# GpSimd's block inversion one slot later, and N made by VectorE in four operations from the exponential

## What is computed

```python
def step(S, inp):
    qt, kt, vt, gt, bt = inp
    S = S * jnp.exp(gt)[:, None, None]
    kv = jnp.einsum('hk,hkv->hv', kt, S)
    delta = (vt - kv) * bt[:, None]
    S = S + kt[:, :, None] * delta[:, None, :]
    o = jnp.einsum('hk,hkv->hv', qt, S)
    return (S, o)
```

## Time and profile before

| | |
|---|---|
| median of 3 runs | 3036.22 us (3026.62 to 3046.79) |
| the profiled execution | 3028.94 us, span 3027.2 us |
| PE busy | 2794.9 us, 92% |
| VectorE busy | 2181.0 us, 72% |
| ScalarE busy | 1812.3 us, 60% |
| GpSimd busy | 1565.5 us, 52% |
| mean granted TensorE clock | 0.971 of full speed |

### The profile page before, as it was taken

One profiled execution on the slowest core, in us unless ns is written; L12 is line 12 of the kernel. 1 busy time (PEld: TensorE's weight loads), 2 busy tenths in 40 slices (PEclk: granted clock), 3 DMA queues, 4 the chain that ended last, 5 costly groups with the idle time before them and its releaser, 6 DMA issues. The chain is left out here.

```text
span 3027.2 us, 75586 instructions
## 1 busy us (share of the span) xinstructions
PE 2794.9 (92%) x24303; PEld 1909.6 (63%) x24303; DVE 2181.0 (72%) x4677; ACT 1812.3 (60%) x6310; POOL 1565.5 (52%) x3737
## 2 busy tenths in 40 slices
PE   5999489999999999999999999999999999869998
PEld 4556256666666666666666666666666666655555
DVE  3443468878877887877778778877788788547676
ACT  3321557777766776777677667766677677332332
POOL 1000456667666666666667666766666666410000
PEclk9999789999999999999999999999999999979999
DMA  3000132212222222212122212122222222110000
GB/s 88 1 1 0 28 59 40 45 38 45 42 48 43 49 43 44 49 35 49 35 49 42 54 37 51 39 46 38 45 40 52 42 49 42 24 42 1 8 7 15
DMA packets 485567, 113.74 MB, mean 38 GB/s; under 512 B 423296, under 2 KB 484336, under 8 KB 485168
## 3 DMA queue, kind: packets, MB, share of 16 engines
q1 hardware_dynamic: 485168, 108.76, 18.0%
HBM read 80.63 MB, written 28.06 MB: 36 GB/s over the span
## 5 line engine op out<-in xcount | busy, mean ns | idle before, releaser
L1216 DVE SCALAR_TENSOR_TENSOR S<-S,gs,bank 128x128 f32<-128x128 f32 x1024 | 287.3, 343 | 232.3 <-PE bank L776 228.0
L1247 DVE SCALAR_TENSOR_TENSOR conv<-raw,ckq,conv 128x512 f32<-128x512 f32 x384 | 302.2, 799 | 110.4 <-ACT conv L1001 104.1
L539 POOL TENSOR_TENSOR btmp<-Bk,Tb 64x14 f32<-64x14 f32 (+6 forms) x896 | 339.7, 379 | 66.1 <-POOL Tb L543 0.9
L543 POOL TENSOR_TENSOR Tb<-Tb,btmp 64x14 f32<-64x14 f32 (+6 forms) x896 | 315.2, 352 | 70.9 <-POOL btmp L539 1.3
L986 ACT ACTIVATE sq_gat<-gat 128x128 bf16<-128x128 f32 x512 | 151.8, 297 | 279.2 <-DVE gat L1232 279.2
L1247 DVE SCALAR_TENSOR_TENSOR conv<-raw,cv,conv 128x512 f32<-128x512 f32 x384 | 291.6, 772 | 12.2 <-ACT conv L1001 7.3
L528 POOL TENSOR_TENSOR Tb<-Bk,lower 64x256 f32<-64x256 f32 x64 | 56.0, 875 | 434.8 <-issue 429.0
L1020 ACT ACTIVATE gatn<-gat,ty 128x128 f32<-128x128 f32 x512 | 163.5, 390 | 181.3 <-POOL ty L518 181.3
L733 PE MATMUL bank<-xnT,wkq 128*128 128x512 f32 x512 | 255.8, 623 | 11.6 <-POOL mkX L425 10.7
L749 PE MATMUL bank<-wz_h,xnT 128*128 128x256 f32 x1024 | 260.6, 401 | 0.0
L819 PE MATMUL bank<-wout_h,gT 128*128 128x256 f32 x1024 | 257.0, 394 | 0.0
(11 more groups left out here) (354 smaller groups left out, 6660.1 us busy)
## 6 DMA issues: line engine op xcount, KB each, us to landing
rowb<-decay_rows SPq DMA_DIRECT2D x256, 64.0 KB, 3.9
blk_n<-N SPq DMA_DIRECT2D x256, 64.0 KB, 2.5
Tp<-blk_t SPq DMA_DIRECT2D x128, 128.0 KB, 2.9
Wp<-blk_w SPq DMA_DIRECT2D x128, 128.0 KB, 3.0
wkq<-in_L_attn_W_qkvz_dram SPq DMA_DIRECT2D x32, 128.0 KB, 2.3
wv<-in_L_attn_W_qkvz_dram SPq DMA_DIRECT2D x16, 256.0 KB, 3.6
Bk<-blk_n SPq DMA_DIRECT2D x64, 64.0 KB, 2.6
blk_t<-Tb SPq DMA_DIRECT2D x64, 64.0 KB, 2.5
```

The source lines that it names most:

```text
L539: pool.tensor_tensor(tmp, Bk[:, j, j + 1:].unsqueeze(2).broadcast_to([64, 15 - j, j]), Tb[:, j, 0:j].unsqueeze(1).broadcast_to([64, 15 - j ...
L543: pool.tensor_tensor(Tb[:, j + 1:, 0:j], Tb[:, j + 1:, 0:j], tmp, ALU.subtract).then_inc(row_rdy, 1)
L1216: i = dve.scalar_tensor_tensor(out=S[:, 2 * b + v, :], in0=S[:, 2 * b + v, :], scalar=gs[t.c][:, kind, 2 * h + v:2 * h + v + 1], in1=pKU[b ...
L1247: dve.scalar_tensor_tensor(out=y, in0=raw[h][:, j, :, :, k:k + H].rearrange("p c b n -> p (c b) n"), scalar=cw[:, j, k:k + 1], in1=y, op0= ...
```

## The change

GpSimd's `base_first` moves from lag 2 to lag 3 and `base_rest` from lag 4 to lag 5, so the first half now stands in even slots and the second in odd ones; x16 stays at lag 6. SP's `base_out` moves with `base_rest`, and `dump` goes ahead of it in the body. The tile ETn, the stage `scaled` and its semaphore are gone. VectorE's `strict` now makes N from ET in four operations of 128x64, one for each u, with CC as the scalar and the Gram matrix as the second operand. ScalarE's `expo` waits for the previous N in place of the previous ETn. Some waits of `base_start` get their values from registers set beforehand.

```diff
--- before.py
+++ after.py
@@ -145,7 +145,6 @@
         rowb = [sb(f"rowb{r}", [P, U, H]) for r in range(2)]
         ET = sb("ET", [P, U, H])
         ETm = sb("ETm", [P, U, H])
-        ETn = sb("ETn", [P, U, H])
         lower = sb("lower", [64, 16, 16])
         N = [sb(f"N{r}", [P, U, H]) for r in range(RING)]
         attn = [sb(f"attn{r}", [P, U, H]) for r in range(RING)]
@@ -217,7 +216,7 @@
         (gs_rdy, ET_rdy, halo_rdy, sse_rdy, nrm_rdy, nn_rdy, der_rdy, o1_rdy, o2_rdy, o3_rdy, sc_rdy) = (
             ev(n) for n in ("gs_rdy", "ET_rdy", "halo_rdy", "sse_rdy", "nrm_rdy", "nn_rdy", "der_rdy",
                             "o1_rdy", "o2_rdy", "o3_rdy", "sc_rdy"))
-        lower_rdy, ETn_rdy, le4_rdy = ev("lower_rdy"), ev("ETn_rdy"), ev("le4_rdy")
+        lower_rdy, le4_rdy = ev("lower_rdy"), ev("le4_rdy")
         rowb_in, rel_rdy = [ev(f"rowb{r}_in") for r in range(2)], ev("rel_rdy")
         base_in, tmp_rdy, row_rdy, base_rdy = ev("base_in"), ev("tmp_rdy"), ev("row_rdy"), ev("base_rdy")
         ln_st, ln_mv, ln_ve, ln_rs, ln_xn, ln_tp, ln_out = (ev("ln1_" + n) for n in (
@@ -342,7 +341,7 @@
 
                 def base_out(s):
 
-                    t = s.back(4)
+                    t = s.back(S_F + 3)
                     if not t.live or t.c % 2:
                         return
                     rows, made, before, sent, solved = (held(sp, v) for v in (
@@ -399,8 +398,8 @@
                     out_weights(s)
                     decays(s)
                     value_weights(s)
+                    dump(s)
                     base_out(s)
-                    dump(s)
                 pipeline(sp, body)
                 sp.wait_ge(t_in, 32 * PAIRS)
                 sp.wait_ge(w_in, 32 * PAIRS)
@@ -472,17 +471,6 @@
                     wait(pool, attn_rdy, t.done(1))
                     pool.tensor_tensor(ETm[:], ET[:], le4[:], ALU.mult).then_inc(ET_rdy, 1)
 
-                def scaled(s):
-
-                    t = s.back(S_F)
-                    if not t.live:
-                        return
-                    pool.wait_ge(exp_rdy, t.done())
-                    pool.wait_ge(der_rdy, t.done())
-                    wait(pool, N_rdy, t.done(1))
-                    pool.tensor_tensor(ETn[:], ET[:], ty[t.c][:, CC, :].unsqueeze(2).broadcast_to([P, U, H]),
-                                       ALU.mult).then_inc(ETn_rdy, 1)
-
                 def halo(s):
 
                     t = s.back(S_P)
@@ -519,7 +507,8 @@
 
                 def base_start(t):
 
-                    read, sent = held(pool, t.pairs(16, 16)), held(pool, t.pairs(16))
+                    read, sent, begun, ones = (held(pool, v) for v in (
+                        t.pairs(16, 16), t.pairs(16), t.pairs(2, 1), t.pairs(2, 2)))
                     pool.wait_ge(m["made"], 2)
                     pool.wait_ge(blk_in, read)
                     wait(pool, t_out, sent)
@@ -527,9 +516,9 @@
 
                     pool.tensor_tensor(Tb[:], Bk[:].rearrange("p j i -> p i j"), lower[:], ALU.mult).then_inc(base_in, 1)
                     pool.wait_ge(m["made"], 2)
-                    pool.wait_ge(base_in, t.pairs(2, 1))
+                    pool.wait_ge(base_in, begun)
                     pool.memset(Tb[:].rearrange("p i c -> p (i c)")[:, ::17], 1.0).then_inc(base_in, 1)
-                    pool.wait_ge(base_in, t.pairs(2, 2))
+                    pool.wait_ge(base_in, ones)
 
                 def base_row(t, j):
 
@@ -544,7 +533,7 @@
 
                 def base_first(s):
 
-                    t = s.back(S_F)
+                    t = s.back(S_F + 1)
                     if not t.live or t.c % 2 == 0:
                         return
                     base_start(t)
@@ -578,7 +567,6 @@
                     halo(s)
                     out_scale(s)
                     derive(s)
-                    scaled(s)
                     causal(s)
                     base_rest(s)
                     base_first(s)
@@ -948,7 +936,7 @@
                     if not t.live:
                         return
                     act.wait_ge(rel_rdy, t.done())
-                    wait(act, ETn_rdy, t.done(1))
+                    wait(act, N_rdy, t.done(1))
                     wait(act, ET_rdy, t.done(1))
                     act.activation(ET[:], rowb[t.c % 2][:], ACT.Exp, scale=-1.0).then_inc(exp_rdy, 1)
 
@@ -1185,13 +1173,16 @@
                     t = s.back(S_F)
                     if not t.live:
                         return
-                    dve.wait_ge(ETn_rdy, t.done())
+                    dve.wait_ge(exp_rdy, t.done())
+                    dve.wait_ge(der_rdy, t.done())
                     dve.wait_ge(gram_mm, t.done())
                     wait(dve, x16_mm, t.done(RING))
                     wait(dve, n_out, t.at(32, 32 - 32 * RING))
-                    split = lambda a: a.rearrange("p (s v) n -> p s v n", s=2)
-                    dve.tensor_tensor(split(N[t.c % RING][:]), split(ETn[:]),
-                                      pGram[:, :, 0, :].unsqueeze(2).broadcast_to([P, 2, 2, H]), ALU.mult).then_inc(N_rdy, 1)
+                    for u in range(U):
+                        i = dve.scalar_tensor_tensor(out=N[t.c % RING][:, u, :], in0=ET[:, u, :],
+                                                     scalar=ty[t.c][:, CC, u:u + 1], in1=pGram[:, u // 2, 0, :],
+                                                     op0=ALU.mult, op1=ALU.mult)
+                    i.then_inc(N_rdy, 1)
 
                 def attention(s):
```

## The result

The changed kernel takes 3236.48 us, median of 4 runs (3234.66 to 3240.95), against 3031.42 (3016.51 to 3046.79, 4 runs) for the kernel before on the same chip: 1.0678 times as long, interval 1.0621 to 1.0735. It is slower by 6.8%. 3245 was forecast, the range was 3120 to 3330.

What follows compares the result with a forecast made beforehand. TensorE was taken as the bound in odd slots (16.9 us), GpSimd's late out_scale lengthening even ones (19.0). Pairs +166 us, with heads +211, on 3028.9 gave 3240, plus 7 for the median: 3245, range 3120 to 3330.

Steps and rivals of the forecast that it cites:

- The mechanism: TensorE's stop in even slots moves from solve(1) to x16, some 2.7 us, with DMA or issue as releaser.
- The rival that Tp would be in time: Tp's load lands before x16, a pair takes 34.15 us, 2925 us in all; chance 0.07.
- The stop at x16: TensorE in even slots waits at x16 for the load of Tp: 2.7 us, once a pair, 64 times.
- signs of being wrong: Second half under 7 us, Tp landing under 5 us after T's last row, or GpSimd held back before out_scale.
- The four operations: VectorE's N in four operations takes 0.86 us, where one took 0.41; an odd slot grows by 0.35 us.
- the rival of 4 x 0.41: VectorE's four operations for N don't overlap and take 1.64 us: 77 us more, 3320 us; chance 0.08.
- The clock: TensorE's granted clock may fall behind the x16 stop, costing 0 to 3.5 us more in even slots; 1.6 taken.
- The pairs without a head: An odd and an even slot together take 38.45 us against 35.86, +2.6, 64 times, 166 us.
- The heads: Weights queue behind Tp, Wp and Bk on SP; TensorE stops at project(0) 3.0 us, 15 heads, 45 us.
- The sum: Whole kernel: pairs 166 us, with the heads +211 on 3028.9, so 3240; 7 for the median, so 3245.
- How the numbers follow: Whole-kernel times for other x16 stops and clock costs: 3095, 3145 and 3370 us; range 3120 to 3330.
- What the shift takes away: Late out_scale in even slots goes; by this alone an even slot falls to 16.9 us, worth 2.0 us a pair.

Runs made afterwards that it cites:

- w_early: Changed kernel with SP's base_out moved to the next body, behind a new head's weights; 3160.44 us, 1.0471 of before.
- late_only: Kernel before with only the change's timing: inversion one slot later, dump ahead of base_out, ETn and one-operation N kept; 3322.3 us, 1.1023 of before.
- n_only: Changed kernel with the inversion back at old lags and dump behind base_out; N in four operations, no ETn; 3005.15 us, 0.9964 of before.
- n_only_late16b: late16b with the inversion back at its old lags and SP's old order; 3036.39 us, 1.0068 of before.
- late16b: Changed kernel with w_early's SP order, x16, w1, w2 later, gated-output transposes ahead of solve(1); 3002.98 us, 0.9922; again 3000.25 us, 0.9944.

## Why the prediction was right

- **The mechanism.** Right. The stop moved from solve(1) to x16, with the DMA of Tp as its releaser, 64 times. The rival that Tp would be in time needed a second half under some 6 us; it took 8.3.
- **The stop at x16.** 2.7 forecast, 2.87 measured. It came out of misses that partly cancel, so its closeness is in part luck. I moved ETm into ETn's place and let it keep its 1.18; it took 0.72 there and started 0.2 earlier, so the second half started at + 7.04, not + 7.69. But the second half took 8.27 (1148.38 to 1156.65), not the 7.99 of the earlier trace rows. So T's last row ended at + 15.31, where I had + 15.7, and the second load (18.54 from the rows above, half of 1.28 behind the first) landed some 3.0 later. The slot shown stops for 2.44; the 42 even slots without a new head between slots 16 and 128 stop for 2.67 on average (2.2 to 3.4), and the longest stops, at the start (10.7) and at heads (3.97), lift the mean to 2.87. None of the signs of being wrong came: 8.27 is over 7, and Tp landed 6.3 after T's last row, not under 5. The stop of 1.2 that the prediction works out from the Trainium skill (DMA: Bandwidth & Descriptors, Anatomy of one DMA) didn't come: its 2.0 us, given there for DMAs that GpSimd issues, is short of the 2.53 and 3.0 that these took from SP.
- **The four operations.** 0.86 forecast, 0.84 measured: 

```profile
1149.13 0.84 DVE L1182 SCALAR_TENSOR_TENSOR N<-ET,ty,bank 128x64 f32<-128x64 f32 x4
```

  The odd slot is 17.23 on average, 17.25 forecast. They overlap, as those on S do, and the rival of 4 x 0.41 fell.
- **The clock.** Forecast as a mean of 1.6 for every pair. In fact, of the 42 even slots of other pairs 18 kept it (19.5 to 20.4 us) and 24 lost it (21.1 to 23.5), at stops of nearly one length, as the stretches above show (2.44 and 2.52). The mean even slot of these pairs is 20.92 against 21.2. Over the steady slots the granted clock is 0.95 (before 0.99); 0.93 was forecast.
- **The slack before.** The prediction says that a whole slot lay between the landing of Tp and x16. It was less, 13.2 us of a slot of 16.9 (next section), and those 3.7 are the stop; the sum, which went from row to row, had it right.
- **The pairs without a head.** 38.15 against 35.54 before: + 2.6, as forecast. I had 38.45 and 35.86, each 0.3 too high: the first by the clock's 1.6, the second since the heads of before are in its mean. The two misses cancel in the difference.
- **The heads.** 3.0 forecast a piece, 3.6 measured: a head's pair grew by 6.2, another by 2.6. The stop at project(0) is 2.5, shorter than the 3.0, but the stop at x16 is longer in these slots too (3.14 on average against 2.67; 3.97 in the one shown) and the clock is lower (0.79 to 0.87 in all 14). w_early agrees on where it comes from: without the queue a head's even slot is only 0.5 longer than another. The step that failed is the assumption that 15 heads add a stop and nothing else.
- **The sum.** 211 forecast, 207.8 in the spans, 205 in the medians. That it came so close is luck in part. The heads cost 54, not 45, while the 8 pairs outside slots 16 to 128 grew by 11 in all, where my way of counting gives them 25 (8 x 2.6 and a head's 3.6): at the start the stops at x16 stand partly in the place of waits at values, line 699, which fell from 34.5 to 20.3 there. I counted ETn's 0.61 as what N's part saves on the chain but not ETm's 0.5, and late_only shows 1.06 for both. For the same reason my expectations of late_only were too low. And the other sums under "How the numbers follow" stand about 8 above what their terms give with the 7 of the median (3087, 3139 and 3362, not 3095, 3145 and 3370), which changes nothing in the range.
- **What the shift takes away.** I gave the late out_scale 2.0 us a pair. The wait at solve(1) fell from 90.9 to 4.8 us, and out_scale starts 1.4 into the even slot, not 4.1, so the shift does remove it. But it is worth 2.0 only alone: even slots are over their odd ones by 2.0 in the kernel before, 1.06 in n_only and 0.67 in n_only_late16b, as a shorter GpSimd chain and cover ahead of solve(1) each seem to take a part of it. With the shift as well, late16b has 0.36. That is why late16b gains 36 us by it and not 64 x 2.0, and 11 of the 28 us between those two spans lie ahead of slot 16.

## What to carry to other kernels

When work moves one stage later in a pipeline, take the slack between the landing of its result and the reader, and subtract the stage's length: before, Tp landed 13.2 us ahead of x16 (1085.02 + 0.64 + 2.9 against 1101.78), a slot is 16.9, and the missing 3.7 is the 3.89 of late_only; less the 1.4 of N's part it is near the 2.44 of the changed kernel. If it doesn't reach, ask whether the reader can stand later before judging the shift: the same shift cost 5.2% with x16 at + 2.0 and gained 1.2% with it at + 5.1. Then count what the reader's new place costs by itself: n_only_late16b stands 1.0% above n_only (1.0068 and 0.9964), which eats nearly all of the gain. And the worth of a shorter operation depends on whether it stands on the path: N's part gave 0.4% under one timing and 3% under the other (1.1023 to 1.0678).

## What the runs showed that I had not expected

GpSimd's ETm, 128x256 in float32, takes 1.18 or 1.28 us beside VectorE's taps and 0.72 away from them. All uses in one row each, minimum, median and maximum in ns, first and last start. Before:

```profile
L473 POOL TENSOR_TENSOR ETm<-ET,le x128: 716/1178/1288, 337.8 to 2596.0; 128x256 f32<-128x256 f32 x128
```

After:

```profile
L472 POOL TENSOR_TENSOR ETm<-ET,le x128: 719/727/734, 336.3 to 2798.5; 128x256 f32<-128x256 f32 x128
```

In the kernel before, ETm mostly starts behind ETn just after VectorE has started a tap; in the changed one it ends as the tap starts (tap at 1148.42, ETm 1147.69 to 1148.41):

```profile
1148.42 0.79 DVE L1238 SCALAR_TENSOR_TENSOR conv<-raw,cv,conv 128x512 f32<-128x512 f32 x1
```

The tap reads two operands from SBUF. The Trainium skill, SBUF — State Buffer, section on SBUF's two separate sides, says that a VectorE operation with two SBUF inputs and a GpSimd operation that reads SBUF hold the shared port pair for a whole instruction each, so that the loser waits until the other is done. The trace agrees: in the kernel before, ETm is 0.46 longer where 0.59 of the tap is left at its start (68 times, as at 1073.26 in the earlier trace rows) and 0.57 longer where 0.70 is left (52 times); in the other 8 it starts ahead of a tap or meets none and takes 0.72. In the changed kernel GpSimd's operation on 64x54 at 1148.73, inside the tap, takes 0.62 where that of 1148.38, ahead of it, takes 0.27. An operation's place against the other engine's taps decides its duration, so the duration of before isn't kept by one that moves.

The clock was the second surprise. Stops of 2.44 and 2.52 us ended once at a granted 1.00 and once at 0.92 over the slot, and in 24 of 42 slots it fell. A stop of this length can't be said to be harmless, nor to cost, and its length doesn't tell which: the clock stayed at 1.00 with a stop of 3.17 and fell with one of 2.21. The even slot behind a new head's lost it at 13 of 14 heads, the others in 11 of 28; in w_early, where the stop at project(0) is gone, it was 8 of 14 and 18 of 28. In late16b, with stops of at most 1.3 us in these slots, none lost it. How much of the 6.8% is the clock and how much the stop itself was not separated by a run. As an estimate, a granted mean of 0.95 over 2205 us is at most 110 us of lost work, and 0.987 over 2008 us before at most 26 (less where TensorE stood anyway): so at most some 84 of the 196.8 are the clock.
